# Reciprocals of three sequences applied during attention, and one planned order for out-projection, routing and scattering

## The reference

```python
x = x + attention(layernorm(x))     # 16 heads of 8, causal, ALiBi bias, then @ Wo + bo
x = x + experts(layernorm(x))
# attention: softmax(q k / sqrt(8) + bias) v, for each of 4 sequences
# experts, over N = 4096 tokens, E = 8, C = 512:
probs = softmax(x @ Wr + br); gate = max(probs); idx = argmax(probs)
pos = (cumsum(one_hot(idx)) * one_hot(idx)); dropped where pos >= C
out[token] = gate * (relu((gate * x[token]) @ W1[idx] + b1[idx]) @ W2[idx] + b2[idx])
```

## Time and profile before

| | us |
|---|---|
| median of 3 runs (lowest, highest) | 735.17 (734.15, 739.01) |
| profiled execution | 729.13 |
| its span, first to last instruction | 727.0 |

### The profile page before, as it was taken

How to read it: one execution, slowest core, us unless ns; L and a number is a source line. 1 busy time by engine, 2 the same in 40 slices (tenths; PEclk the granted TensorE clock), 3 DMA queues, 4 the chain that set the end, 5 groups by cost and what they waited for, 6 DMA issues and landing times. The chain is left out here.

```text
span 727.0 us, 13826 instructions
## 1 busy us (share of the span) xinstructions
PE 543.3 (75%) x4933; PEld 255.0 (35%) x4933; DVE 493.9 (68%) x964; ACT 440.7 (61%) x800; POOL 243.1 (33%) x403
## 2 busy tenths in 40 slices
PE   2775889889988988998898899876777029036774
PEld 1441333232333333333323323213666027024553
DVE  4999779789888988888897888600686306116544
ACT  1970468678877877787787788771244105007773
POOL 2651121221221122122114422210125744758552
PEclk9895699999999999999999999975885559658997
DMA  7488436432304322442432040001112124112012
GB/s 171 109 179 250 112 98 166 100 89 50 83 18 101 81 66 53 108 91 73 96 79 54 6 83 10 9 5 39 45 58 71 54 96 172 32 48 82 16 44 58
DMA packets 64906, 57.30 MB, mean 79 GB/s; under 512 B 12209, under 2 KB 55590, under 8 KB 64828
## 3 DMA queue, kind: packets, MB, share of 16 engines
q1 hardware_dynamic: 56152, 50.15, 27.9%
q10 hardware_dynamic: 6128, 2.90, 1.6%
q0 software_dynamic: 2560, 3.39, 1.4%
HBM read 29.40 MB, written 29.69 MB: 81 GB/s over the span
## 5 line engine op out<-in xcount | busy, mean ns | idle before, releaser
L799 DVE TENSOR_REDUCE neg_max<-bank 128x2 f32<-128x1024 f32 (+2 forms) x320 | 342.9, 1114 | 64.2 <-PE bank L723 62.2
L820 ACT ACTIVATE probs<-ring 128x512 f32<-128x512 f32 (+4 forms) x481 | 302.1, 681 | 83.1 <-PE ring L751 69.9
L751 PE MATMUL ring<-q_operand,k_operand 56*128 56x512 bf16 (+3 forms) x768 | 166.5, 337 | 18.6 <-ACT probs L820 14.5
L772 PE MATMUL sums<-probs,v_all 128*9 128x512 f32 (+3 forms) x1536 | 165.6, 504 | 2.1 <-POOL probs L853 1.5
L853 POOL TENSOR_SCALAR_AFFINE_SELECT probs<-probs 128x512 f32<-128x512 f32 x128 | 80.2, 635 | 220.7 <-ACT probs L820 220.1
L723 PE MATMUL bank<-k_operand,q_operand 54*128 54x512 bf16 (+3 forms) x768 | 145.8, 341 | 7.0 <-DVE v_all L525 5.3
L751 PEld LDWEIGHTS ring<-q_operand,k_operand 56*128 56x128 bf16 x768 | 50.4, 94 | 155.4 <-ACT probs L820 111.0
L717 PE MATMUL bank<-masks 64*128 64x128 bf16 (+2 forms) x768 | 72.5, 225 | 5.3 <-DVE neg_max L799 4.9
L1310 PE MATMUL ring<-sel,ident 128*128 128x256 f32 x50 | 17.4, 525 | 58.6 <-DMA x_rows<-ye,rows 31.1
L723 PEld LDWEIGHTS bank<-k_operand,q_operand 54*128 54x128 bf16 x768 | 46.2, 97 | 24.6 <-DVE neg_max L799 15.1
L717 PEld LDWEIGHTS bank<-masks 64*128 64x128 bf16 x768 | 36.9, 96 | 38.4 <-DVE neg_max L799 25.8
(11 more groups left out here) (154 smaller groups left out, 684.5 us busy)
## 6 DMA issues: line engine op xcount, KB each, us to landing
q_operand<-q_rows SPq DMA_DIRECT2D x64, 96.0 KB, 3.7
k_operand<-k_rows SPq DMA_DIRECT2D x32, 192.0 KB, 4.3
q_rows<-qk_parts SPq DMA_DIRECT2D x36, 128.0 KB, 2.4
k_rows<-qk_parts SPq DMA_DIRECT2D x36, 128.0 KB, 2.4
expert_rows<-fill SPq DMA_DIRECT2D x16, 258.0 KB, 5.1
rows<-expert_rows SPq DMA_DIRECT2D x8, 516.0 KB, 7.0
weighted_sums<-osum SPq DMA_DIRECT2D x128, 18.0 KB
sums_in<-in_L_attn_x SPq DMA_DIRECT2D x4, 512.0 KB, 7.3
```

Source lines behind the costliest of these rows:

```text
L751: last = nc.tensor.matmul(psS[:, bank, w * j:w * j + w], k_op[rows, buf, p, P * kb:P * kb + P], q_op[rows, buf, c, p, q0:q0 + w], start=Tr ...
L772: last = nc.tensor.matmul(psO[32 * i:32 * i + HD + 1, q0:q0 + w], v_all[:, n, kb, i, :], probs[:, u % NPROBS, i // 2, i % 2, 0:w], start=u ...
L799: nc.vector.tensor_reduce(neg_max[:, n % 2, slot, kc, :, pairs[0]:pairs[-1] + 1, t % CH], src, AX.X, ALU.max, negate=True).then_inc(a_read, 1)
L820: nc.scalar.activation(dst, src, ACT.Exp).then_inc(ring_read, 1)
```

## The change

**During attention,** for sequences 0, 1 and 2: when seven of a group's twelve V units are through (groups 5, 9, 13), VectorE inverts the sequence's denominators between two maxima; SyncE stores the reciprocals to DRAM and loads them back spread over all 128 partitions (512 KB) into a new tile; in the group after, GpSimd multiplies the loaded sums by them, in place, in two halves (`divide`), and adds the bias to the residual rows there too. The bias additions of the last sequence follow those of sequence 2. SyncE clears the slots at every A once the stores are out, and loads the residual rows at groups 4 to 7. `plan()` counts the new work in its times, which moves a few A units by two or three places.

**In the next block,** only the last sequence has its reciprocals spread by TensorE and is divided by VectorE. The others are projected at once. The projection has four PSUM banks instead of two, the spread reciprocals one. A list scheduler (`route_plan`) puts all items of the stage into `ROUTE_ORDER`, by estimated start and the longest path behind each, and all engines walk that list. The powers of sequences 0 to 2 come in one instruction of 8 columns each. `choose` no longer takes the sum of the exponentials and its reciprocal (`place` does) and, for sequences 0 to 2, keeps a running count of chosen tokens per expert (`seen`), so that the counts of a sequence need no multiplications over the earlier ones: 9 at most in place of up to 32. The ten multiplications without use before the stage are gone. The last four tiles are scaled by VectorE, the others by ScalarE. The bodies of `choose` and `place` are otherwise as before and have moved into a class `Router`; the working tiles of the stage lie in one buffer `early`, which held the projected q and k before.

```diff
+EARLY = B - 1
+EARLY_AT = {6: ["reciprocals"], 7: ["store_reciprocals"], 9: ["load_reciprocals"], 20: ["divide"], 21: ["divide"],
+            23: ["bias"], 24: ["bias"]}
+EARLY_TIME = {"reciprocals": ("dve", 960), "divide": ("pool", 1250), "bias": ("pool", 1200)}
...
+            b = (n - H // GH - 1) // (H // GH)
+            tick = (n - H // GH - 1) % (H // GH) * NU + u
+            for name in EARLY_AT.get(tick, []) if 0 <= b < EARLY else []:
+                order.append(("E", n, name, b, int(name in EARLY_AT.get(tick - 1, []))))
+                engine, time = EARLY_TIME.get(name, (None, 0))
+                dve += time * (engine == "dve")
+                pool += time * (engine == "pool")
...
+                def store_reciprocals(b):
+                    sp.wait_ge(rden_ready, b + 1)
+                    sp.dma_start(rden_dram[b].rearrange("h (j q) -> (h j) q", q=P), den[:, b, :]).then_inc(rden_out, 16)
+
+                def load_reciprocals(b):
+
+                    if b == 0:
+                        for i in range(B - 1):
+                            sp.wait_ge(parts_out[i], 16 * NSTORE)
+                    else:
+                        sp.wait_ge(at_ready, QC * b)
+                    sp.wait_ge(rden_out, 16 * (b + 1))
+                    sp.dma_start(r["rdb"], rden_dram[b].unsqueeze(0).to_broadcast([HD, H, S])).then_inc(rdb_in, 16)
...
-                    elif kind == "A" and n >= 5 and args[0] % 8 == 4 and clears:
+                    elif kind == "A" and clears:
...
-                        if 7 <= n < 7 + B:
-                            load_residuals(sp, n - 7)
+                        if 4 <= n < 4 + B:
+                            load_residuals(sp, n - 4)
...
+                def reciprocals(b):
                     dve.wait_ge(o_in[b], 32)
                     nc.vector.reciprocal(den[:, b, :], den[:, b, :]).then_inc(rden_ready, 1)
...
+                def divide(b, c):
+                    pool.wait_ge(o_in[b], 32)
+                    pool.wait_ge(rdb_in, 16 * (b + 1))
+                    to = slice(CW * c, CW * c + CW)
+                    nc.gpsimd.tensor_tensor(ot[:, b, to], ot[:, b, to], r["rdb"][:, to], ALU.mult).then_inc(at_ready, 1)
...
+                            if b == EARLY - 1 and c == QC - 1:
+                                for last in range(QC):
+                                    add_bias(EARLY, last)
...
+GROUPS = [(QC * b, QC * b + 1) for b in range(EARLY)] + [(k,) for k in range(QC * EARLY, CHUNKS)]
...
+    items = {("reciprocal", 0): ("dve", 960, LANDED, []), ("fold", 0): ("dve", 900, 1500, [])}
+    group = {k: g for g, ks in enumerate(GROUPS) for k in ks}
+    K0 = QC * EARLY
+    for k in range(CHUNKS):
+        if k >= K0:
+            items["rb", k] = ("pe", 1400, 0, [("reciprocal", 0)] + [("divide", k - 1)] * (k > K0))
+            items["divide", k] = ("dve", 650, 0, [("rb", k)])
+        items["project", k] = ("pe", 1350, 0, [("divide", k)] * (k >= K0) + [("add", k - 4)] * (k >= 4))
+        items["add", k] = ("dve", 2300, 0, [("project", k)])
+        items["apply", k] = ("act", 1700, 0, [("scales", group[k])])
+        items["turned", k] = ("pe", 1250, 0, [("apply", k)] + [("take", k - 2)] * (k >= 2))
+        items["columns", k] = ("act", 600, 0, [("turned", k)] + [("logits", k - 2)] * (k >= 2))
+        items["logits", k] = ("pe", 1300, 0, [("columns", k)])
+        items["take", k] = ("dve", 220, 0, [("logits", k)])
+    for g, ks in enumerate(GROUPS):
+        items["power", g] = ("pool", 250 + 780 * len(ks), 0, [("add", ks[-1])])
...
+        items["power", g] = ("pool", 250 + 780 * len(ks), 0, [("add", ks[-1])])
+        items["scales", g] = ("dve", 800, 0, [("power", g)])
+    for r in range(B):
+        items["choose", r] = ("dve", 2000, 0, [("take", QC * r + QC - 1)])
+        items["exps", r] = ("act", 280, 0, [("choose", r)])
+        items["counts", r] = ("pe", 1200, 0, [("choose", r), ("fold", 0)] + [("place", r - 1)] * (r > 0))
+        items["place", r] = ("dve", 2100, 0, [("counts", r), ("exps", r)])
+        items["gated", r] = ("act", 3200 if r < EARLY else 1600, 0, [("place", r)])
+        if r == EARLY:
+            items["gated_last", 0] = ("dve", 1300, 0, [("place", r)])
+        for u in range(KB * r, KB * r + KB):
+            items["send", u] = ("pool", 1280, 0, [("gated", r)] if u < TILES - CH else [("gated_last", 0)])
+    followers = {i: [] for i in items}
+    for i, (_, _, _, after) in items.items():
+        after += [(i[0], j) for j in [i[1] - 1] if (i[0], j) in items]
...
+    while len(order) < len(items):
+        ways = []
+        for i, (engine, time, at, after) in items.items():
+            if i not in done and all(a in done for a in after):
+                start = max([free[engine], at] + [done[a] + (HOP if items[a][0] != engine else 0) for a in after])
+                ways.append((start, i))
+        first = min(ways)[0]
+        start, i = max((w for w in ways if w[0] <= first + SOON), key=lambda w: height(w[1]))
+        free[items[i][0]] = done[i] = start + items[i][1]
+        order.append(i)
+    return order
+
...
-        def power(k):
-            pool.wait_ge(ve2_ready, k + 1)
-            c = slice(CH * k, CH * k + CH)
-            nc.gpsimd.tensor_tensor(rs2[:, c], ve2[:, c], half_pow[:, 0:CH], ALU.pow).then_inc(pw2_ready, 1)
+        def power(g):
+            ks = GROUPS[g]
+            pool.wait_ge(ve2_ready, ks[-1] + 1)
+            c = slice(CH * ks[0], CH * ks[-1] + CH)
+            nc.gpsimd.tensor_tensor(rs2[:, c], ve2[:, c], half_pow[:, 0:CH * len(ks)], ALU.pow).then_inc(pw2_ready, 1)
...
-        for k in range(CHUNKS):
-            power(k)
         pool.wait_ge(slots_clear, 16 * E * CAP // (2 * P))
         pool.wait_ge(tok_ready, 1)
-        for u in range(TILES):
-            send_rows(u)
+        for name, i in ROUTE_ORDER:
+            if name == "power":
+                power(i)
+            elif name == "send":
+                send_rows(i)
         pool.wait_ge(x1_out, 16 * CHUNKS)
...
-            pe.wait_ge(at_ready, k + 1)
-            if k >= 2:
-                pe.wait_ge(x1_ready, k - 1)
+            if k >= K0:
+                pe.wait_ge(at_ready, k + 1)
+            if k >= 4:
+                pe.wait_ge(x1_ready, k - 3)
...
-        idle_work(psT2[0], 10)
-        pe.wait_ge(rden_ready, B)
-        reciprocals(0)
-        reciprocals(1)
```

421 lines of the change are left out of this document (242 added, 179 removed).

## The result

The changed kernel took 715.39 us (median of 4 runs, 712.62 to 715.78) against 737.09 us for the kernel before (4 runs, 734.15 to 740.22): a ratio of 0.970, interval 0.964 to 0.975. The forecast was 716.0 in 710.5 to 723.5, and faster by over 1%. The time fell where it was forecast, but the traces say that this was in part luck: errors of opposite sign nearly cancel, an attention that ended earlier than forecast and results of TensorE that came late.

The account below looks back on a forecast made before the run. GpSimd's queue order, holding the 32 scatters behind eight powers, was taken to bound the stage after attention. Terms: -22.7 + 1.5 + 1.5 + 0.5 = -19.2 us, from the median 735.17 to 716.0; 8-in-10 range 710.5 to 723.5.

Parts of the forecast that it names:

- What bounded the stage: Stage after attention: GpSimd's queue order, eight powers ahead of all scatters, then 31 steps of 1.28 us.
- First send at 528.0 for an opening at 502.2: Stage after attention: first scatter at 528.0 us, once VectorE reaches `place` of sequence 0.
- Last send at 569.7: Stage after attention: last scatter starts at 569.7 us instead of 592.4, a gain of 22.7 us.
- TensorE at the low clock, the rival of 719.5: Stage after attention: TensorE stays at low clock, last start slips to 572.2, 2.5 to 4 us back; chance 0.15.
- the 2.1 us of lateness: Stage after attention: with TensorE at 1.2 GHz all through, the last batch of scatters has its data 2.1 us late.
- Sends stretched beside VectorE, 720.8: Stage after attention: about 20 VectorE instructions each hold a scatter for 0.24 us, 4.8 us in all; chance 0.05.
- The early reciprocals wait for their load, 739: Attention: early reciprocals wait for the loaded sums, stalling VectorE and TensorE three times; 739 at 9 us each; chance 0.03.
- Attention +3.5: Attention: added work costs 1.5 for reciprocals, 1.5 for GpSimd's work and 0.5 for SyncE; block opens at 505 to 506.
- another 1.5: Attention's tail: GpSimd's division and bias additions for sequence 2 make masks late; 1.5 us taken, bounds 0 to 3.8.
- the third term: Attention, SyncE: earlier clearing writes and residual loads stand ahead of rows of maxima; 0.5 us taken, bounds 0 to 2.
- The rest, 134.6, unchanged: Chain behind the last scatter: 134.6 us, which the change leaves alone.
- The base: Whole kernel before: profiled execution 729.13 us, median 735.17; the 6 us offset is kept, turning 709.9 into 716.0.

Follow-up runs that it names:

- chips Q and R: Two chips of the follow-up runs; the kernel before, unedited, has medians of 725.84 us and 726.95 us there.
- the kernel above: Changed kernel with the eight bias additions back where the kernel before had them, ahead of the last four groups' first masks; 703.23 us.
- the one with the held tokens: Changed kernel with its 32 sends of tokens held until all eight experts are done, by one more wait on GpSimd; 715.18 us.
- chip P: Chip of the first follow-up group; the changed kernel, unedited, took 716.53 us there against 735.22 for the kernel before.

## Why the forecast was right, and where it was not

Step by step, against the profiles on chips Q and R and the two of the kernel before without late results:

- **What bounded the stage** (the queue order, then 31 x 1.28): shown. Five moved sends alone gave -6.9 us where -6.4 was expected, and all powers first put the first send 15.4 us later and made the kernel 8.7 us slower.
- **First send at 528.0 for an opening at 502.2**: 25.8 forecast, 25.6 in all seven profiles that have the changed order and no idle multiplications. The list of VectorE's blocks holds.
- **Last send at 569.7**: 67.5 forecast, 67.5 measured in all five profiles of the changed order on chips Q and R. The stage gave 90.2 - 67.5 = 22.7 us. About 9 of it come from the early division (the two kernels without it: 76.5). The other 13.7 come from the new order with the idle multiplications left out; in that order they would put the sends back by 4.5, in the old one they stood in the way for 0.65 at most.
- **TensorE at the low clock, the rival of 719.5**: its condition came true in the kernel above and in the one with the held tokens, its price did not. Granted 0.50 over the whole stretch, data for the 25th send were there in time; the 2.1 us of lateness in that working were a little too dear.
- **Sends stretched beside VectorE, 720.8**: no. VectorE was busy for 29.65 of 55.5 us of the last window, and the sends kept 1.28. The rule of the Trainium skill (SBUF — State Buffer, section Who interferes with whom), by which VectorE's two-port modes starve the descriptors of GpSimd's DMAs, gives no price here that the spacing shows; the trace decides.
- **The early reciprocals wait for their load, 739**: no. None of the three waited for a DMA.
- **Attention +3.5, the step that failed ("opens at 505 to 506").** The term was sized too high, and the start from which it was counted, 502.2, was not a fixed one. Windows from the first maximum of group 4 to the last maximum, and from there to the opening: the kernel before, the changed kernel on chip R, and the one with the held tokens on chip Q, whose attention is the changed kernel's (the third number from the end is the granted clock):

```profile
161.24:465.02 303.78, 274.35 (x3045) 96.58 (x3041) 257.37 (x252) 242.18 (x407) 78.18 (x153) 1.00 0.28 63
465.02:502.19 37.17, 25.65 (x178) 4.92 (x175) 3.70 (x5) 22.14 (x36) 6.62 (x12) 0.74 0.06 11
```

```profile
159.74:464.03 304.29, 274.36 (x3045) 96.42 (x3041) 259.62 (x256) 242.21 (x407) 78.55 (x153) 1.00 0.29 65
464.03:499.11 35.08, 23.02 (x179) 5.24 (x175) 1.21 (x2) 21.95 (x36) 13.61 (x18) 0.82 0.05 11
```

```profile
158.16:462.41 304.25, 274.35 (x3045) 96.36 (x3041) 259.52 (x255) 242.19 (x407) 78.54 (x153) 1.00 0.29 66
462.41:495.36 32.95, 20.53 (x179) 4.95 (x175) 1.22 (x2) 21.91 (x36) 13.61 (x18) 0.94 0.05 13
```

  The first window repeats to 0.1 us: 304.2 to 304.3 in all six executions of the changed kernel's attention, 303.8 to 303.9 in the three of the old one, 303.5 and 303.6 without the early division. So three reciprocals, their way through memory and the four divisions ahead of the last maximum cost 0.7 to 0.8 us, and the whole change 0.5 us, in the loop; the forecast had 1.5 for the reciprocals alone. In the tail, where it had another 1.5, nothing is seen to be paid: 32.9 to 35.1 us in the changed kernel, 35.0 to 37.2 before. The tail's length goes along with its granted clock, within one kernel too: 32.9 at 0.94, 34.2 at 0.89, 35.1 at 0.82 in the changed one, 35.0 at 0.87 and 37.2 at 0.74 in the old one.

  Ahead of group 4, where the clearing writes of the third term begin, executions of one kernel differ as much (first maximum of group 4 at 158.2 to 161.6, before 158.8 to 161.3). Together the same attention opened the block anywhere from 495.4 to 500.1 in the changed kernel and from 497.7 to 502.3 in the kernel before, and both profiles of the old order without late results, the forecast's base among them, lie at the late end. Most of the earlier opening therefore can't be put down to the change. The timed medians on chip R say the same: 726.95 - 702.36 less 22.7 for the stage and 0.4 for the rest leaves 1.5 us by which attention got shorter, with an interval of 2 us to either side. Whether the change itself keeps the clock of the tail up is open. Further work there is paid: four more divisions made it 37.6 us at 0.89, 3.5 more for 5.1 us of work.
- **The rest, 134.6, unchanged**: 134.2 in the changed kernel on chip R and 134.6 to 137.2 in the edits on chips Q and R that leave it as it is, longer where its granted clock was lower (0.81 for 134.2, 0.75 and 0.76 for 136.4 and 137.2). With late results 138.6 to 141.2 (before, with the five sends moved: 142.4).
- **The base.** The forecast took 6 us as the offset from the profiled 729.13 to the median 735.17 and kept it. By the later runs that offset fits what late results cost the old kernel (which chip each of the first runs had is not known): 728.81 and 729.13 are the times of executions without them, and chips Q and R have medians of 725.84 and 726.95. They seem to cost the changed kernel more: 716.53 on chip P against 702.36 on R is 14.2 us, and for the kernel before 735.22 - 726.95 = 8.3 us. This puts the whole difference between two chips down to them; of the 14.2 us the profiles show 7.2 up to the last send and 4.4 in the rest of the profile from chip P. The first of these stands in the timeline: in the new order the last power waits in GpSimd's queue between two sends, so lateness in the chain of spread, division and projection (7.2 us from opening to last send, 74.7 against 67.5) goes straight into the sends; with all powers first no gap is left among the sends (81.0 on chip P is what the first send and 31 spacings give). So of 24.6 us that the change brings on a chip without late results, 18.7 to 21.7 are left on one with them.

The forecast's -19.2 was thus composed of a stage that was exact, an attention term some 3 us too high, counted from an opening at the late end of what the same attention gave, and late results that it did not have (some 3 to 6 us of the gain). The first errors made the forecast too high, the last one made it too low, and that they nearly cancelled was luck.

## What to carry to other kernels

Before a profile is taken as the base of a sum, compare its time with the timed runs: the 6 us of difference here fit, by the later runs, a chip with another behaviour, and a change that reorders a queue answers to that behaviour too. Before a difference between two profiles is put down to an edit, look for a stretch that repeats: the opening of the block differed by up to 4.7 us between executions of one and the same attention, the loop inside it by 0.1. When the sends of an in-order queue bound a stage, count from the moment when the first may start, and look at what each instruction placed among them waits for: a power between two sends was free on two chips and cost 5 us on the third. Idle time of an engine in a dense loop is not free cover: 10.2 us more on GpSimd, busy for 35% of the span, cost 7 us in attention, and on VectorE the first 2.7 us cost under 1, the next 5.4 cost 6.2 before the last maximum.

## What the runs showed of the hardware

On the chip of the first result and on chip P, in each of five profiles, TensorE's semaphores were updated 0.6 to 12 us after the engine's records ended (other engines waited up to 14.4 us for one), at nearly the same places of the program: from the middle of the rows' stage (in the order with all powers first, hardly before the experts, 0.6 us) and in the experts. Nothing is late in attention. On chips Q and R none of eight profiles shows it, and neither does the first profile of the kernel before. Whether the multiplications ran slowly or their completion was told late, the records don't say. The ends of records are modelled, and two updates that must lie eight multiplications apart came 0.1 us apart: the last count of the third sequence (record over at 533.56) at 543.79, the projection behind it (record over at 543.76) at 543.88, by TensorE's semaphores. That fits a late report better than slow work, but it was not tested. The low clock alone is not the cause: on chip R nearly the whole stage ran at 0.50 in one kernel with nothing late. A link with GpSimd's sends is neither shown nor excluded: in the five profiles the first late update of the experts comes 5.0 to 5.8 us after the first send of tokens, and the first one in the rows' stage 7 to 12 us after the first send of rows, but the same sends run on chips Q and R without any, and the kernel that was to test the link ran on chip Q. The cause stays open. Chip P is 8 us slower than R in the kernel before (of 735) and 14 us in the changed one (of 716).
